# Cross-attention and FP4 feed-forward kernel: an order of their own for ACT, DVE and POOL in the first two tiles, and a leaner setup

## The reference, cut to what matters

```python
def reference(x, ctx_768, Wq, Wk, Wv, Wo, bo, w_gate, w_up, w_down):
    # x (4, 1024, 256), ctx (4, 154, 192), 16 heads of 64, ffn width 704
    h = layernorm(x)
    q, k, v = heads(h @ Wq), heads(ctx_768 @ Wk), heads(ctx_768 @ Wv)
    attn = softmax(q @ k.T * 64 ** -0.5)
    x = x + (heads_back(attn @ v) @ Wo + bo)
    h = layernorm(x)
    gate = fp4_linear(h, w_gate)          # both operands quantised, blocks of 16
    h = silu(gate) * fp4_linear(h, w_up)
    return x + fp4_linear(h, w_down)

def fp4_quant_dequant(x):                 # on activations and on weights
    scale = max(max(abs(x), over 16) / 6, 1e-12)
    return nearest_of(0, .5, 1, 1.5, 2, 3, 4, 6; abs(x / scale)) * sign(x) * scale
```

## Time and profile before

| | |
|---|---|
| Time, median of 3 | 902.29 us (901.35 to 903.94) |
| The profiled execution: its own time / its span | 904.46 us / 902.3 us |
| Busy PE | 842.0 us (93%), 6278 matmuls |
| Busy DVE / ACT / POOL | 710.2 (79%) / 523.1 (58%) / 539.2 us (60%) |
| DMA, mean | 26 GB/s, 23.14 MB |
| Chain that ended last | PE 68%, DVE 20%, issue 4%, ACT 4%, POOL 2%, DMA 1% |

### The profile page before, as it was taken

The page is one execution under the profiler, slowest core; times in us unless marked ns, Lnnn a source line. Parts: engine busy times, 40 slices in busy tenths (PEclk is TensorE's granted clock), DMA queues, the critical chain, the costliest instruction groups (busy, mean ns, idle before and its releaser), DMA issues.

```text
span 902.3 us, 19161 instructions
## 1 busy us (share of the span) xinstructions
PE 842.0 (93%) x6278; PEld 807.9 (90%) x6278; DVE 710.2 (79%) x2157; ACT 523.1 (58%) x1878; POOL 539.2 (60%) x810
## 2 busy tenths in 40 slices
PE   4887899999999999999999999999999999999986
PEld 4766789999988999999988999999988999999876
DVE  5659788877777888887877888886877888887787
ACT  4554466665665565657655665666665665665531
POOL 6438776765644666665553666665644566666643
PEclk9889999999999999999999999999999999999999
DMA  8101000001010000001010000000100000000000
GB/s 243 38 23 44 7 19 7 24 14 47 8 36 19 13 25 13 25 13 42 13 35 21 13 18 14 24 14 12 49 7 19 12 15 23 14 18 14 7 7 18
DMA packets 20137, 23.14 MB, mean 26 GB/s; under 512 B 2658, under 2 KB 18250, under 8 KB 20042
## 3 DMA queue, kind: packets, MB, share of 16 engines
q1 hardware_dynamic: 20042, 21.94, 8.0%
HBM read 17.74 MB, written 4.19 MB: 24 GB/s over the span
## 4 chain that ended last, share of the span: by engine, by line
PE 68%; DVE 20%; issue 4%; ACT 4%; POOL 2%; DMA 1%; SPq 0%; DVEq 0%; ACTq 0%
PE ps_q L1161 10%; PE ps_g L1246 9%; PE ps_s L1203 9%; PE ps_t L1213 6%; PE ps_o L1226 5%; PE ps_o L1228 5%; PE ps_o L1227 5%; PE ps_g L1124 3%; DVE pT_lo L737 3%; DVE scales L764 3%; DVE negmax L884 3%; PE ps_m L1260 2%; PE ps_m L1262 2%; PE ps_m L1261 2%; PE ps_m L1089 2%
## 5 line engine op out<-in xcount | busy, mean ns | idle before, releaser
L511 POOL TENSOR_TENSOR probs<-probs,rsum 128x308 f32<-128x308 f32 x256 | 179.7, 702 | 260.6 <-DVE rsum L848 260.1
L678 ACT ACTIVATE probs<-ps_s,negmax 128x154 f32<-128x154 f32 x512 | 194.8, 386 | 217.7 <-DVE negmax L884 216.5
L884 DVE TENSOR_REDUCE negmax<-ps_s 128x2 f32<-128x308 f32 x256 | 121.0, 473 | 90.7 <-PE ps_s L1203 89.9
L1226 PE MATMUL ps_o<-B_sb,pT_lo 128*128 128x256 f32 x640 | 180.9, 283 | 0.9 <-DVE x_both L939 0.6
L1228 PE MATMUL ps_o<-B_sb,pT_hi 128*128 128x256 f32 x640 | 180.7, 282 | 0.0
L1227 PE MATMUL ps_o<-B_sb,pT_hi 128*128 128x256 f32 x640 | 180.4, 282 | 0.0
L737 DVE TENSOR_TENSOR pT_lo<-ps_t,pT_hi 128x256 fp32r<-128x256 f32 (+1 forms) x256 | 122.8, 480 | 34.4 <-ACT pT_hi L572 34.0
L1213 PE MATMUL ps_t<-ident,probs 128*128 128x128 f32 x640 | 113.6, 276 | 25.0 <-DVE pT_lo L737 21.9
L1246 PE MATMUL ps_g<-WGU,xqT_hi 128*128 128x352 f32 x504 | 131.8, 343 | 2.0 <-DVE B_sb L737 1.7
L1226 PEld LDWEIGHTS ps_o<-B_sb,pT_lo 128*128 128x128 f32 x640 | 121.0, 189 | 1.4 <-issue 0.8
L1228 PEld LDWEIGHTS ps_o<-B_sb,pT_hi 128*128 128x128 f32 x640 | 121.4, 190 | 0.0
(11 more groups left out here) (228 smaller groups left out, 2218.3 us busy)
## 6 DMA issues: line engine op xcount, KB each, us to landing
xa<-in_x_dram SPq DMA_DIRECT2D x33, 128.0 KB, 2.1
xr<-in_x_dram SPq DMA_DIRECT2D x32, 128.0 KB, 2.0
out_dram<-y_xn SPq DMA_DIRECT2D x30, 128.0 KB, 1.7
W_sb<-in_L_xattn_Wk_dram SPq DMA_DIRECT2D x4, 512.0 KB, 3.7
W_sb<-in_L_xattn_Wv_dram SPq DMA_DIRECT2D x3, 512.0 KB, 3.3
probs<-in_L_xattn_Wq_dram SPq DMA_DIRECT2D x2, 512.0 KB, 8.6
Wo_sb<-in_L_xattn_Wo_dram SPq DMA_DIRECT2D x1, 1024.0 KB, 9.7
VT<-in_L_ffn_w_down_dram SPq DMA_DIRECT2D x2, 352.0 KB, 3.8
```

The source lines that it names most:

```text
L511: pool.tensor_tensor(unit, unit, rsum[:, 2 * u:2 * u + 2].unsqueeze(2) .to_broadcast([P, 2, M]), ALU.mult).then_inc(norm_p, 1)
L678: ins = act.activation(probs[:, h, 0:M], ps_s[k % 2][:, s * M:(s + 1) * M], ACT.Exp, bias=negmax[:, h:h + 1], accum_out=sums[:, h:h + 1])
L884: dve.tensor_reduce(negmax[:, 2 * k:2 * k + 2], ps_s[k % 2][:, 0:UM].rearrange("p (h m) -> p h m", h=2), AX_X, ALU.max, negate=True).then_ ...
L1226: pe.matmul(ps_o[:, 0:C], lo[:, j, :], w[:, 0:C], start=first, stop=False)
```

## The change

What it does, part by part:

- **Order.** `schedule` calls a new function `first` for tiles 0 and 1 on ACT, DVE and POOL; PE keeps `step`. In `first`, ACT, DVE and POOL take in slot k what PE leaves in slot k, in PE's order: the scores of pair k, their sums and product (pair k, not k-1), the probabilities of pair k-2, the queries, then the jobs and the turned chunk of the same slot.
- **Chunks.** Chunk 0, which was quantised in the setup, now begins in slot 0 of tile 0, and all the others move (`RAW_AT`, `TURN_AT`). DVE's division stands between largest score and sums, POOL's rounding is split: two of its instructions in one slot, the third in the next. The second layernorm of tile 0 (`rstd` on POOL, `layer_norm2_out` on ACT, `x_scales` on DVE) keeps its slots, 4 and 5 of tile 1.
- **Setup.** One key job before tile 0, not two; the other three in slot 0, each into a bank of its own, and after them the transposes of the last three context tiles. The context has 192 columns, and these are cut into 96 + 96 rows, not 128 + 64, so that ACT copies a tile with one instruction, not three, and two memsets of DVE go. POOL clears K's two parts each behind one layernorm. PE starts with 12 products of the identity with itself, and has 4 more before the transposes of x (`warm`).
- **Loads.** Only two of five context tiles, a quarter of Wk and the rest of Wk come before the first chunk; Wq comes in four parts on ACT's own queue; Wv is loaded in two halves, at the second and the fourth key job; Wo, the third chunk and bo stand behind those. In later batches a weight is one load of 192 rows, not of 128 with the rest kept in SBUF.

```diff
+                first(0, ("start", 0))
+                first(1, ("settle", 0))
...
-            "start": {0: [("K", 2, "0"), ("K", 3, "1")], 1: [("V", 0, "0"), ("V", 1, "1")],
+            "start": {0: [("K", 1, "1"), ("K", 2, "t"), ("K", 3, "o")], 1: [("V", 0, "0"), ("V", 1, "1")],
...
-        RAW_AT = [None, 0, 2, 4, 6, 8, 11, 14]
-        TURN_AT = [1, 3, 5, 7, 9, 12, 14, 15, 18, 19]
+        RAW_AT = [0, 1, 3, 5, 7, 10, 11, 14]
+        TURN_AT = [3, 4, 7, 8, 10, 13, 14, 15, 18, 19]
...
+            sp.dma_start(ctx_raw[:, 0:2, :], ctx_rows[0:2 * P, :].rearrange("(r p) c -> p r c", p=P)).then_inc(ld_ctx, 16)
+            load_w_cols(Wk, slice(0, 2 * P), ld_wk)
+            load_w_cols(Wk, slice(2 * P, INNER), ld_w)
             load_raw(0)
...
+            sp.wait_ge(k_mm, 2)
+            load_w_cols(Wv, slice(0, INNER // 2), ld_wv)
+            sp.wait_ge(k_mm, KV)
+            load_w_cols(Wv, slice(INNER // 2, INNER), ld_w)
             sp.dma_start(Wo_sb[:, :, :], Wo.rearrange("(q p) n -> p q n", p=P)).then_inc(ld_wo, 16)
             load_raw(2)
...
@@ POOL
-            pool.memset(K_sb[0][:, :, :].bitcast(F32), 0.0).then_inc(kpad_p, 1)
...
             for n in range(2):
                 rstd(mv1, rs1, nm1, (ln1_v, 3 * n + 3), ln1_p, 4 * n)
-            pool.memset(K_sb[1][:, :, :].bitcast(F32), 0.0).then_inc(kpad_p, 1)
+                pool.memset(K_sb[n][:, :, :].bitcast(F32), 0.0).then_inc(kpad_p, 1)
...
+            def first(t, setup):
+                for k in range(SLOTS):
+                    normalise(t, k)
+                    if raw_at(t, k, 2) is not None:
+                        round_chunk(raw_at(t, k, 2), (2,))
+                    if t == 0 and k == 0:
+                        rstd(mv1, rs1, nm1, (ln1_v, 9), ln1_p, 8)
+                    if raw_at(t, k, 1) is not None:
+                        round_chunk(raw_at(t, k, 1), (0, 1))
+                    if k == 1:
+                        add_bias(t)
...
+                    if t == 1 and k == 4:
+                        rstd(mv2, rs2, nm2, (ln2_v, 3), ln2_p, 0)
@@ ACT
+            for i in range(4):
+                cols = slice(i * 2 * P, (i + 1) * 2 * P)
+                act.dma_start(Wq_raw[:, :, cols], Wq[:, cols].rearrange("(k p) n -> p k n", p=P)).then_inc(ld_wq[i], 16)
...
+            def first(t, setup):
+                for k in range(SLOTS):
+                    exponentials(t, k)
...
+                    if k >= 2:
+                        weights_hi(t, k - 2)
+                    elif t == 1:
+                        weights_hi(0, k + PAIRS - 2)
+                    if t == 1 and k == 5:
+                        layer_norm2_out(0)
...
+                    if q_unit(t, t, k) is not None:
+                        q_hi_part(t, q_unit(t, t, k))
+                    for job in jobs_at(setup, k):
+                        take_hi(job, 0)
...
@@ DVE
+            def first(t, setup):
+                for k in range(SLOTS):
+                    largest_score(t, k)
+                    if raw_at(t, k, 1) is not None:
+                        chunk_divide(raw_at(t, k, 1))
+                    invert_sums(t, k)
+                    if raw_at(t, k, 1) is not None:
+                        chunk_rounder(raw_at(t, k, 1))
+                    if k >= 2:
+                        weights_lo(t, k - 2)
...
+                    if t == 1 and k == 5:
+                        x_scales(0)
+                    if raw_at(t, k, 0) is not None:
+                        chunk_scales(raw_at(t, k, 0))
...
+                    for job in jobs_at(setup, k):
+                        take_lo(job, 0)
+                    if turn_at(t, k, 0) is not None:
+                        chunk_lo(turn_at(t, k, 0))
@@ PE
+            warm(12)
+            pe.wait_ge(ld_ctx, 16)
+            context_transposes(range(2))
+            pe.wait_ge(pre_ev, 2)
+            make(("K", 0, FIRST_K[0]), 0)
+            warm(4)
             pe.wait_ge(xln1_a, 2)
             m_free(None, (xT_lo, 1))
             both_transposes(ps_m)
```

More of the change, by code:

```diff
@@ L178, in some, with schedule @@
             return not isinstance(count, int) or count > 0
-        def schedule(eng, step, finish):
-            step(0, 0, before=False, gate=False, down=False, out_=False, setup=("start", 0))
-            step(0, 1, gate=False, down=False, out_=False, setup=("settle", 0))
+        def schedule(eng, step, finish, first=None):
+            if first:
+                first(0, ("start", 0))
+                first(1, ("settle", 0))
+            else:
+                step(0, 0, before=False, gate=False, down=False, out_=False, setup=("start", 0))
+                step(0, 1, gate=False, down=False, out_=False, setup=("settle", 0))
             step(1, 0, down=False, out_=False)
@@ L521, in step @@
                 for k in range(SLOTS):
-                    if before and k == 0:
+                    if before and k == 0 and e > 1:
                         normalise(e, PAIRS - 1)
@@ L649, in step @@
                 for k in range(SLOTS):
-                    if before and k < 3:
+                    if before and k < 3 and (e > 1 or k > 0):
                         weights_hi(e, k + PAIRS - 3)
@@ L674, in step @@
                     if own:
-                        act.wait_ge(max_v, PAIRS * t + k + 1)
-                        for s in range(2):
-                            h = 2 * k + s
-                            ins = act.activation(probs[:, h, 0:M], ps_s[k % 2][:, s * M:(s + 1) * M], ACT.Exp,
-                                                 bias=negmax[:, h:h + 1], accum_out=sums[:, h:h + 1])
-                        ins.then_inc(exp_a, 1)
-                    if isinstance(t, int) and t == 0 and k == 1:
-                        layer_norm1_out(2, 0)
+                        exponentials(t, k)
                     if own and ahead and k == 4:
@@ L794, in layer_norm1 @@
                 stats(xa[par][:, :], st1, mv1, rs1, (ld_xa[par], 16 * pairs), ln1_v, 3 * n)
-            for half in range(2):
-                h = slice(D - D * half, P - D * half)
-                dve.memset(ctxT[h, 1 + half, :], 0.0).then_inc(cpad_v, 1)
             def wq_lo_part(i):
@@ L1072, in finish @@
                 add_y(T, ps_s[1])
-            schedule(dve, step, finish)
+            schedule(dve, step, finish, first)
         @block.tensor
```

263 lines of the change are left out of this document (150 added, 113 removed).

## The result

The changed kernel takes 907.35 us, the median of 6 runs (906.01 to 909.07), against 901.82 us for the kernel before in 6 runs beside it (900.97 to 903.94): a ratio of 1.0056, with a 95% interval of 1.0039 to 1.0074. I had forecast 896.5 and a gain; the time lies outside my range. The profiled execution took 907.14 us (span 905.4), near its median, where the one of before stood 2.6 us above the median of these runs. So the two profiles differ by only 3 us, and the rest is in which executions were profiled.

What follows compares the result with a forecast made beforehand. Loads were taken to bound the start, PE tile 0 and DVE tile 1. The terms -5.8 - 7.0 + 7.0 = -5.8 us took the profiled 904.46 to 898.7, a median of 896.5; forecast's own range 893 to 899.5, 8-in-10 range 889.5 to 903.5.

Steps and rivals of the forecast that it cites:

- tile 1's term: Tile 1, bound by DVE: 27.4 us would grow to 34.4, 7.0 us more, bounds 2 and 11 more.
- Tile 2 ... 0, within 1 either way: Tile 2: chunk 7 further along but the first tile's fp4 rounding behind it, so no change, within 1 us.
- The waits for sums, 5.2 us: Tile 1: DVE waits for ACT's sums, four slots at 1.0 and four at 0.3 us, nothing covering them.
- The second layernorm, forecast 2.2 us of wait: Tile 1: POOL's first two chunk 6 instructions stand ahead of it, so DVE's x_scales wait 2.2 us, 1.1 more.
- DVE's work in tile 1, forecast +1.3: Tile 1: one more division, +1.5 us, one more chunk low part, +0.5, minus the last B job, -0.7.
- The gaps that I had vanish (0.6): Tile 1: 0.6 us of DVE's present small gaps would vanish.
- Tile 0, forecast -7.0: Tile 0: 39.6 us against 46.6, so 7.0 us less; 11 less if PE and DVE overlap well, 3 less if badly.
- The start, forecast 16.4: Setup: first query product at 12.8 us, first scores at 16.4, 5.8 us less, bounds 3 to 8 less.
- the 8.4 that I had as its latest: Setup loads: Wk's quarter lands at 8.4 us if all of Wq goes first; 7.0 was taken.
- 1 (waits cost little): Waits cost little as ACT is ahead: tile 1 takes 28 to 29 us, 890.5 us in all; chance 0.18.
- 2 (a slow start): Setup loads at half rate leave 2 of the start's 5.8 us: 900.5 us, no change to tell; chance 0.19.
- Rival 3: Tile 1: PE's clock stays down, granted clock below about 0.65, tile 1 takes 43 us, 905 us; chance 0.13.

Runs made afterwards that it cites:

- e1: Changed kernel with the reciprocal of the sums and POOL's division by them moved to the next slot's head in both tiles; 907.2 us, ratio 1.0057.
- e2: Changed kernel with POOL doing tile 0's second layernorm and fp4 rounding ahead of chunk 6's and 7's first rounding steps; 904.4 us, ratio 1.0026.
- e3: Changed kernel with tile 1 put back in the order of the kernel before, new order in tile 0 alone; 901.1 us, ratio 0.9992.
- e14: Changed kernel with tile 1's sums and weights' copies one slot later, plus POOL's layernorm and fp4 rounding first as in e2; 902.4 us, ratio 1.0000.
- e11: e3 with chunks 2 to 5 back in the slots of the kernel before; 897.2 us, ratio 0.9933.
- e6: Changed kernel without the 4 identity products behind the first key job; 907.9 us, ratio 1.0054.
- e12: Changed kernel with 12 more unread PE products in each of slots 1 to 7 of tile 1; 907.0 us, ratio 1.0047.
- e13: Changed kernel, new order in both tiles, with chunks 2 to 5 back in the slots of the kernel before; 905.1 us, ratio 1.0028.
- e10: e8 with chunks 2 to 5 back in the slots of the kernel before; 904.4 us, ratio 1.0021.
- e8: Changed kernel with the old order in both tiles and POOL's bias added in slot 3 of tile 0; 902.5 us, ratio 0.9989.

## Why the prediction was wrong

The four terms in the profiles: start -4.6 (forecast -5.8), tile 0 -5.4 (-7.0), tile 1 +10.0 (+7.0), tile 2 +2.6 (0); with 0.4 at the end this makes +3.0 instead of -5.8. The directions of the first three were right, and the mechanisms in part. **The step that failed is tile 1's term, "27.4 + 1.3 + 5.2 + 1.1 - 0.6 = 34.4", with "Tile 2 ... 0, within 1 either way" behind it**: together they were 5.6 us too small, and the gains ahead of them 2.8 too large. By what DVE did between tile 1's borders, the 10.0 us are 7.3 more of waits (1.6 to 8.9; the term had 5.2 + 1.1), 2.3 more of busy time (25.18 to 27.47; the term had 1.3) and 0.4 more of small gaps (the term had 0.6 less).

- **The waits for sums, 5.2 us.** Measured 5.2, in 7 waits: five of 0.9 and two of 0.3, where I had four of 1.0 and four of 0.3; that the sum is the same to a tenth is luck. The size was right, and yet it is not a cost of its own: without it (e1) nothing came back, because DVE then meets ACT one instruction later. The sum of DVE's waits says more: 8.9 us in after (1.0056), 8.5 in e1 (1.0057), 5.8 in e2 (1.0026), 3.3 in e3 (0.9992). It does not say all: e14 has the 5.8 of e2 and is 2.3 us faster, and why stays open.
- **The second layernorm, forecast 2.2 us of wait, measured 3.1.** I had the right queue, but left out a product by the sums and chunk 5's third step that stand in it too. With tile 2 it is the best-shown single part: e2 gave back 2.7 us.
- **DVE's work in tile 1, forecast +1.3, measured +2.4 (27.24 against 24.81).** I counted the division and a low part. Tile 0 had left work over as well (below). Instructions stretched beside POOL add little to the difference, since the kernel before has them too. The gaps that I had vanish (0.6) did not.
- **Tile 0, forecast -7.0.** I measured tiles by PE, and PE ran ahead of DVE. This is DVE's first largest score of tile 1, after and before:

```profile
63.22 0.47 DVE L916 TENSOR_REDUCE negmax<-ps_s 128x2 f32<-128x308 f32 x1
```

```profile
70.54 0.47 DVE L884 TENSOR_REDUCE negmax<-ps_s 128x2 f32<-128x308 f32 x1
```

- It comes 4.4 us after PE's first scores of tile 1, where it came 1.8 after the earlier trace rows. So 2.6 of the 9.9 us that PE had gained were owed by DVE and paid in tile 1, the tile that DVE bounds. Measured on DVE, from its first largest score of tile 0 (24.20 before, 19.65 after) to that of tile 1, tile 0 gained 2.8 us, not 5.4. And the chunks' later slots moved one more division, rounding and low part across the same line: by e11 against e3, 3.9 us by the medians and 5.3 by the ratios, a part of it stretched instructions and not moved ones. I had priced that move at 2 us (1.5 + 0.5) and never asked whether it had to be made.
- **The start, forecast 16.4, came at 17.64.** POOL's clearing released ACT as said, but at 10.9 instead of 10.2, since x landed at 3.5, not 2.8. Then the chain left the path that I had followed (start us, us, what):

```profile
2.14 6.86 DMA W_sb<-in_L_xattn_Wk_dram
...
9.13 1.45 PE ps_g L1199 x8
10.58 1.71 PE ps_q L1268 x8
12.29 0.87 PE ps_m L1184 x4
...
13.18 0.60 ACT xT_hi L600
...
13.81 0.70 DVE xT_lo L790
...
14.55 0.99 PE ps_q L1252 x6
```

- My path had no transposes of x and no high part of x in it, and nothing for the 4 identity products, which stood 1.71 us in front of the transposes; the first query came at 14.55, not 12.8. By e6 the 4 are no loss all the same, since without them POOL's clearing ends last. The 12 I had at 2.7 us; they took 5.4 (1.53 to 6.93), and cost nothing, as the context landed only at 7.5. Wk's quarter landed at 9.00, beyond the 8.4 that I had as its latest. The rate was not at fault. These are the busy times of the first 10 us, which answer to the earlier trace rows:

```profile
0.00:5.00 5.00, 3.47 (x16) 3.47 (x17) 0.60 (x3) 1.28 (x1) 1.49 (x12) 1.00 0.60 166
5.00:10.00 5.00, 3.44 (x21) 3.01 (x21) 1.30 (x4) 2.26 (x5) 4.76 (x8) 1.00 1.03 284
```

- By 9.0 us, 166 x 5 + 284 x 4 = 1.97 MB had moved, more than the 0.64 MB up to that quarter and all 1.05 MB of Wq. By queue it was 0.98 MB on SP's and 1.02 on ACT's. So some 0.3 MB of what SP had issued behind the quarter moved before the quarter's last byte did. My bound had taken the loads of a queue to move one after the other.

Of the rivals, 1 (waits cost little) and 2 (a slow start) did not happen. Rival 3 named the right tile and the right sign, with the wrong mechanism: PEclk was 0.86, above its 0.65, and e12 gives no sign that the clock counts. What I lacked was a rival in which DVE's and POOL's waits are paid in full and tile 0's gain is only borrowed.

The slower kernel is thus explained by two things, by the ratios: the new order in tile 1, 5.8 us (e3), most of it by POOL's queue and the meetings with ACT together (e14, 5.1 us), and the chunks' new slots, 5.3 us more (e11 on e3; on the changed kernel as it is, e13, 2.5; with the old order in both tiles, e10 on e8, the new slots are the better ones by 2.9). With both taken back, e11, the rest of the change is 6 us faster than the kernel before. What of tile 1's order is left beside e14, about a microsecond, stays open, and so does how much of the slots' price is work moved and how much is instructions stretched, and the exact worth of the 16 products.

## What to carry to other kernels

Measure a stage by the engine that bounds the next one: what the other engines gain by running ahead is a loan. In this kernel the order in which DVE takes its partners' results in the same slot paid where PE was the limit (tile 0, with PE busy for 39 of 47 us; 7.9 us, but only with the old slots) and cost where DVE was (tile 1, 5.8 us); a wait in such a ring is not removed by moving one of its members, so look at the sum of the engine's waits, and at its busy time for the same instructions. And a split instruction block needs a look at who stands behind its first half.
